# A mixture-of-experts block on one core: a waited-for clear after each scatter of GpSimd

## What is computed

```
x = x + attention(layernorm(x))      # linear attention, 16 heads of 8, RMS norms, rotary embedding
x = x + experts(layernorm(x))        # router: the best 2 of 8 experts of each token
x = x + mixing(layernorm(x))         # a recurrence over the 1024 tokens of each batch
x = x + experts(layernorm(x))
```

## Time and profile before

| | us |
|---|---|
| three runs, median | 1330.14 |
| lowest and highest | 1322.95, 1336.12 |
| profiled execution | 1346.64 |
| its span, first to last instruction | 1344.8 |
| busy: TensorE / VectorE / ScalarE / GpSimd | 855.2 / 918.4 / 659.9 / 623.3 |

### The profile page before, as it was taken

One profiled execution on the slowest core, in us unless ns is written; L12 is line 12 of the kernel. 1 busy time (PEld: TensorE's weight loads), 2 busy tenths in 40 slices (PEclk: granted clock), 3 DMA queues, 4 the chain that ended last, 5 costly groups with the idle time before them and its releaser, 6 DMA issues.

```text
span 1344.8 us, 21163 instructions
## 1 busy us (share of the span) xinstructions
PE 855.2 (64%) x5110; PEld 697.5 (52%) x5111; DVE 918.4 (68%) x2976; ACT 659.9 (49%) x1788; POOL 623.3 (46%) x597
## 2 busy tenths in 40 slices
PE   3777777742178887776457667657423777887850
PEld 1665566542177887765123333323223777876750
DVE  5688888645465655555299999999953565655657
ACT  3676666611154444444576766655322444444435
POOL 3024444433545554545215555675434555555440
PEclk9788877856599888899677787787655899889885
DMA  7022222212222222221311222211092222222239
GB/s 223 16 60 79 78 79 80 65 53 68 83 75 74 68 76 69 71 58 49 110 60 63 69 83 86 94 47 38 30 254 66 71 69 75 73 70 69 62 97 315
DMA packets 144880, 111.79 MB, mean 83 GB/s; under 512 B 15779, under 2 KB 135724, under 8 KB 144464
## 3 DMA queue, kind: packets, MB, share of 16 engines
q1 hardware_dynamic: 126928, 77.58, 20.6%
q0 software_dynamic: 17920, 33.88, 7.9%
HBM read 62.84 MB, written 50.64 MB: 84 GB/s over the span
## 4 chain that ended last, share of the span: by engine, by line
DVE 31%; PE 31%; issue 13%; ACT 7%; another core or an unknown queue 5%; POOL 5%; DMA 4%; DVEq 2%; ACTq 1%; SPq 0%; POOLq 0%
PE banks L965 8%; PE banks L946 5%; POOL queue_dram L508 4%; PE banks L948 4%; PE banks L947 4%; DVE rope_c L1414 3%; PE banks L828 2%; PE banks L854 2%; DVE stats L1095 2%; PE banks L955 2%; ACT gated L690 1%; DVE gated L1239 1%; DMA out<-xmid 1%; DVE tile_up L1253 1%
## 5 line engine op out<-in xcount | busy, mean ns | idle before, releaser
L519 POOL DMA_INDIRECT result_dram<-ytile,result_row x288 | 283.9, 986 | 274.3 <-DVE ytile L1259 191.8
L508 POOL DMA_INDIRECT queue_dram<-hffn,place_i x192 | 222.9, 1161 | 205.8 <-DVE place_i L1177 120.6
L946 PE MATMUL banks<-xt_parts,tile_up 128*128 128x256 f32 x584 | 185.8, 318 | 87.4 <-DVE tile_up L1253 81.6
L1239 DVE SCALAR_TENSOR_TENSOR gated<-banks,tile_bias,gated 128x256 f32<-128x256 f32 x292 | 127.8, 479 | 99.9 <-ACT gated L690 76.4
L965 PE MATMUL banks<-wdown_sb,gated 128*128 x1152 | 171.2, 297 | 20.6 <-DVE gated L1239 20.5
L947 PE MATMUL banks<-xt_parts,tile_up 128*128 128x256 f32 x584 | 172.9, 296 | 0.0
L948 PE MATMUL banks<-xt_parts,tile_up 128*128 128x256 f32 x584 | 172.7, 296 | 0.0
L946 PEld LDWEIGHTS banks<-xt_parts,tile_up 128*128 128x128 f32 x584 | 119.9, 205 | 100.7 <-DVE xt_parts L1248 61.9
L965 PEld LDWEIGHTS banks<-wdown_sb,gated 128*128 128x128 f32 x1152 | 157.8, 211 | 24.3 <-issue 24.2
L690 ACT ACTIVATE gated<-banks,tile_bias 128x256 f32<-128x256 f32 x292 | 121.9, 470 | 97.4 <-PE banks L948 70.2
L696 ACT ACTIVATE xt_parts<-banks 128x256 fp32r<-128x256 f32 x150 | 57.8, 386 | 215.2 <-PE banks L955 171.7
(11 more groups left out here) (210 smaller groups left out, 1986.8 us busy)
## 6 DMA issues: line engine op xcount, KB each, us to landing
xtiles<-queue_dram SPq DMA_DIRECT2D x160, 130.0 KB
qkv<-result_dram SPq DMA_DIRECT2D x24, 512.0 KB, 4.3
x_dram<-xres SPq DMA_DIRECT2D x32, 256.0 KB
result_dram<-ytile,result_row POOLq DMA_INDIRECT x288
xin<-x SPq DMA_DIRECT2D x16, 256.0 KB
xold<-x SPq DMA_DIRECT2D x16, 256.0 KB
expo<-w_up SPq DMA_DIRECT2D x2, 2048.0 KB, 9.3
xin<-x_dram SPq DMA_DIRECT2D x16, 256.0 KB
```

The source lines that it names most:

```text
L508: nc.gpsimd.indirect_dma_start(queue_dram, bass.IndirectOffsetOnAxis(ap=place_i[s][:, at:at + 1], axis=0), hffn[s][c][:, j, :], None).then ...
L519: nc.gpsimd.indirect_dma_start(result_dram, bass.IndirectOffsetOnAxis(ap=result_row[i][:, h:h + 1], axis=0), ytile[i][:, h, :], None, boun ...
L946: nc.tensor.matmul(ps_up[at][:, h, :], hi, xt_parts[at][:, 0, :], start=True, stop=False)
L1239: last = nc.vector.scalar_tensor_tensor(gated[at][:, h, :], ps_up[at][:, HCH + h, :], tile_bias[(i + 1) % STEP][:, HCH + h:HCH + h + 1], g ...
```

## The change

After each indirect DMA of GpSimd, in `scatter` and in `experts`, GpSimd sets a scratch tile of 16 columns to zero, waits until that is done and clears the semaphore. The seven waits of `pace` and the semaphore step that follows each are gone. The eight batches of the attention stage are one loop of four rounds.

```diff
+SPACER = 16
+        spacer = sb("spacer", [P, SPACER])
+        spaced = sem("spaced")
-            def pace(m, pair):
-                if pair == 1:
-                    pool.wait_ge(attn_turned[1], m + 1)
...
-                elif pair == 7:
-                    pool.wait_ge(h2_turned[0], m + 1)
-            def scatter(m, s, paced):
+            def space():
+                nc.gpsimd.memset(spacer[:], 0.0).then_inc(spaced, 1)
+                pool.wait_ge(spaced, 1)
+                pool.sem_clear(spaced)
+            def scatter(m, s):
...
                 for c in range(HALVES):
                     for j in range(TPC):
-                        if paced and c + j:
-                            pace(m, c * TPC + j)
-                            pool.sem_inc(place_taken, 1)
                         for k in range(TOPK):
...
                                 hffn[s][c][:, j, :], None).then_inc(queued[s][c], 16)
+                            space()
             def experts(f):
...
                                 ytile[i][:, h, :], None, bounds_check=NO_RESULT - 1, oob_is_err=False).then_inc(y_stored[i], 16)
+                            space()
...
-            with pool.Fori(0, 2) as n:
-                scatter(n * 2 + 1, 1, True)
-                scatter(n * 2 + 2, 0, True)
-            scatter(5, 1, True)
-            scatter(6, 0, False)
-            scatter(7, 1, False)
-            scatter(8, 0, False)
+            with pool.Fori(0, BATCH // 2) as n:
+                scatter(n * 2 + 1, 1)
+                scatter(n * 2 + 2, 0)
             experts(FIRST)
```

More of the change, by code:

```diff
@@ L568, in _ @@
                 next_sums(m - (BATCH - 1))
-                scatter(m, 0, False)
-            scatter(2 * BATCH - 1, 0, False)
-            scatter(2 * BATCH, 0, False)
+                scatter(m, 0)
+            scatter(2 * BATCH - 1, 0)
+            scatter(2 * BATCH, 0)
             experts(SECOND)
```

## The result

The kernel before took 1333.13 us (median of 4 runs, 1322.95 to 1338.26), the changed one 1500.97 us (4 runs, 1497.44 to 1502.11). The ratio is 1.127, 95% interval 1.119 to 1.134: slower, by more than the forecast's 1.105. The changed kernel's profiled execution took 1500.24 us (span 1498.4 us, granted clock 0.774), 153.6 us more than the 1346.64 us of the one before.

The account below looks back on a forecast made before the run. Experts were taken as bound by TensorE and VectorE passing tiles, mixing by VectorE, with attention's scatters mostly unwaited for. Terms summed to +141.3 us on 1346.64 us, ratio 1.105, forecasting 1470 us, range 1400 to 1530.

Parts of the forecast that it names:

- The cost of one clear: GpSimd's scatters: start to start 1.93 us in the queue (+0.67 us), 2.01 us for results (+0.73 us).
- Rival 1: GpSimd's sequencer runs ahead all the same, +0.28 us per scatter, experts stay hidden: 1357 us; chance 0.08.
- rival 3: The wait does not hold, clears finish beside the scatter's own work: 1334 us, no change; chance 0.05.
- Mixing stage: Sums queue behind the scatters: 9.0 us per batch, +45.0 us over five, +9.4 and +8.1 us for batches 15 and 16.
- Expert stages: GpSimd becomes the bound at 4.10 us per tile: +29.3 us in the first stage, +31.4 us in the second.
- rival 2: VectorE holds the clears up, in the experts its copy of weights: another 30 us, 1500 us; chance 0.10.
- Batch 8 to the first experts: Batch 8's last scatter starts 10.0 us later, less 1.9 us from a smaller hole and earlier start: +8.1 us.
- the hole after the first scatter: Batch 8's burst: the 1.98 us hole should shrink to a usual gap, as scatters 5 to 8 run in the loop.
- What bounded the experts before: Expert stages before the change: TensorE and VectorE pass tiles to each other, 3.70 us per tile.
- The dispatcher's price per instruction: GpSimd's software dispatcher: 0.04 us more per clear, some 17 us on the whole change; not used in the sum.
- Rival 4: Faster: spacing gives back ScalarE's 19.6 us of waits in attention batches 7 and 8: 1314 us; chance 0.04.
- The pair waits: Attention stage: five batches lose seven waits each, nothing there is waited for, so 0 us by itself.

Follow-up runs that it names:

- e1: The changed kernel without its clears in the experts, only those behind the queue's scatters kept: 1272.98 us, ratio 1.078 to a before of 1182.3 us.
- e2: The kernel before, pair waits kept, with waited-for clears behind the scatters of results alone: 1401.45 us, ratio 1.186 to a before of 1182.3 us.
- e4: The changed kernel with each clear waited for only ahead of the next one: 1183.08 us, ratio 1.001 to a before of 1182.3 us.
- e6: The changed kernel with each clear replaced by the sequencer's own semaphore count, wait and step kept: 1404.68 us, ratio 1.040 to a before of 1349.42 us.
- e7: The changed kernel with two waited clears after each scatter instead of one: 1626.69 us, ratio 1.205 to a before of 1349.42 us.
- e3: The changed kernel without any clears, so neither clears nor pair waits: 1181.85 us, ratio 1.001 to a before of 1182.3 us.
- e10: The kernel of e3 (neither clears nor pair waits) on another chip: 1401.18 us, ratio 1.041 to a before of 1347.21 us.
- e11: The kernel of e4 (clears waited for one later) on another chip: 1411.47 us, ratio 1.049 to a before of 1347.21 us.
- e5: The changed kernel as it is, run again in another set: 1501.90 us, ratio 1.112 to a before of 1349.42 us.
- e8: The changed kernel with a waited clear only after every second scatter: 1339.63 us, ratio 0.992 to a before of 1349.42 us.
- e9: The changed kernel with clears only after each second scatter of batches 1 to 7 and each fourth in the experts: 1289.82 us, ratio 0.959.

## Why the prediction held, and where its steps were off

The sum was 141.3 us and the profiled executions differ by 153.6. Up to the first result the forecast was 10.7 us too high, in the experts 23.8 us too low, and the rest is within 1.3 us. That two errors of opposite sign half cancel was luck; either alone would have left the total in the range. The ratio is also one for late chips, from whose trace it was worked out: for the other sort e1 and e2 add up to an estimate of some 1492 us, a ratio of 1.26, which no run tested.

**The cost of one clear: right.** I had 1.93 and 2.01 us from start to start; the rows above have 1.89 and 1.98. The mechanism, a stopped sequencer whose next issue lies in the open, is shown from three sides: the same clears without the stop cost nothing (e4), the same wait without an engine to wait for leaves the scatters where they were (e6), and a second clear costs 0.27 us, not another 0.7 (e7). Rival 1 and rival 3 fall with these.

**Mixing stage: right.** Place_i 9 to 15 grew by 53.7 us where 54.4 stood in the sum, 15 to 16 by 8.8 (8.1), the last burst by 8.8 (10.0). VectorE's wait for the sums (11.91 us ahead of 795.38) is the one forecast.

**Expert stages: the right bound, too small a size.** 293.1 us were forecast for the first stage, 305.9 measured. Over all 144 rows: 72 steps inside a tile have a median of 2.01 us, just the forecast's, but a mean of 2.10, with a single step of 4.43 us among them; 63 steps from tile to tile are 2.15 us instead of 2.09; and 8 steps at the end of a loop round are 2.49 us, for which the sum had nothing of its own. That is 6.1 + 3.5 + 3.2 = 12.8 us, of which 3.3 us are clears that VectorE held up (rival 2 below). The second stage is short by 11.0 us in the same way. These two terms are the whole miss upward, 23.8 us.

**Batch 8 to the first experts: wrong, and in the other direction.** I forecast +8.1 us; the first result came 2.6 us earlier. Two steps failed, and they nearly cancel. "Nothing there is waited for, so this gives 0 us by itself" missed that the spacing frees ScalarE and VectorE from late signals: place_i 8 comes 23.9 us earlier. And "it still fits, with 2 us to spare" was reckoned against batches 33.1 us apart; they now come 30.9 to 33.7 us apart, the last one 26.4 us. So GpSimd is full in attention: a batch's first scatter starts 4 us behind its place_i in batch 2 and 13.7 us in batch 8, which waits behind batch 7 (place_i 8 at 307.35, batch 7's last scatter at 318.75). GpSimd's rows, and VectorE's beside them:

```profile
318.75 0.97 POOL L497 DMA_INDIRECT queue_dram<-xtiles,place_i  x1 [1.02 <-issue]
319.07 4.42 DVE L1210 TENSOR_TENSOR up_lo<-expo,up_hi 128x4096 fp32r<-128x4096 f32 x1
...
321.03 3.30 POOL L497 DMA_INDIRECT queue_dram<-hffn,place_i  x1 [1.19 <-issue]
324.33 0.13 POOL L485 MEMSET spacer<- 128x16 f32 x1
327.72 0.97 POOL L497 DMA_INDIRECT queue_dram<-hffn,place_i  x1 [3.26 <-issue]
...
354.27 0.97 POOL L497 DMA_INDIRECT queue_dram<-hffn,place_i  x1 [0.80 <-POOL spacer L485]
370.89 1.00 POOL L509 DMA_INDIRECT result_dram<-ytile,result_row  x1 [15.53 <-DVE ytile L1246]
```

The burst starts 11.4 us earlier than in the earlier trace rows and is 33.24 us long instead of 24.90. These +8.3 us are what I had for the burst, but by another way. The first scatter lies beside a VectorE operation of 4.42 us and takes 3.30; in the kernel before a scatter of this burst met the same operation and took 5.19, so 1.9 us less are lost there now. And the hole after the first scatter, which I had expected to shrink from 1.98 us to a usual gap in the loop, grew to 3.26. The written-out code didn't make it: e3 has batch 8 in the loop and a hole of 1.99 us. Nor did VectorE's operation: in e7 the first scatter takes 0.97 us and the hole is 3.26 us again. What makes it is open.

**What bounded the experts before: wrong.** I read the 3.70 us of a tile as TensorE and VectorE passing tiles to each other. They can make one in 2.5 us, and GpSimd's two scatters allow 2.58 (e3: 191.4 us). The likely rest is late signals: without them the two stages are 142.6 us shorter (e3), and the view of waits over the whole run shows 81.8 us of this kind in them. That the other 61 us are waits that follow from these is argued, not shown. I had read this kind of wait in two attention batches only the earlier trace rows. It didn't spoil the sum, since the changed kernel's experts are bound by GpSimd alone and the forecast went from there; it did hide that with a smaller dose the change could have won.

**Rival 2** (VectorE holds the clears up) had a true mechanism at a fifth of its price. The mean of 0.152 us hides two kinds of clears. Of the 288 in the experts 40 lie beside VectorE's copy of weights (L1240), and 34 of these take 0.31 to 0.45 us; the 61 that lie beside L1226 alone take 0.14, like the others:

```profile
377.82 0.63 DVE L1240 CAST tile_up<-up_lo 128x512 fp32r x1
378.19 0.31 POOL L485 MEMSET spacer<- 128x16 f32 x1
```

Over both stages the 34 cost 6.3 us more than at 0.14 each, where the rival had 30. In the mixing stage six clears take 0.53 to 0.54 us, each beside L1365 or L1366. The page of the Trainium skill that speaks of a shared port lock (SBUF — State Buffer, section Who interferes with whom) has copies among the operations that can hold GpSimd up, and the 34 clears agree. It also lets a VectorE operation on two tiles in SBUF contend with GpSimd's reads; the scatter of 3.30 us beside VectorE's subtraction of 4.42 above agrees. The dispatcher's price per instruction, which I had set beside the sum as an estimate of 0.04 us more per clear (the Trainium skill, GPSIMD Engine Reference, section Instruction dispatch), doesn't show: the queue's steps came out at 1.89 or 1.90 us, under the sum's 1.93, not over it.

**Rival 4** had the mechanism and the wrong sign in total. Bursts do hold up signals to ScalarE and VectorE, spacing frees them, and in attention that is worth 24 us (19.6 forecast). My counter-argument, that these two batches run code for the first time, falls: e3 and e10 are one kernel and differ by 78 us at place_i 8 from chip to chip. At the dose of the change the experts and the mixing stage cost more than six times that gain.

**The pair waits** that I priced at 0 are worth 0 where signals are on time (e3) and most of 54 us in attention where they aren't (e10). The changed kernel has no late wait without them, so its clears seem to do their work, and the 0 came out right by another way than I gave; no run has clears and pair waits both in attention.

## What to carry to other kernels

A wait on one's own engine behind a DMA issue costs little for the instruction waited for and much for the next issue, which can't be prepared: 0.7 us per indirect DMA here. If a spacer or an ordering step is needed, wait for it one step later (e4: free; on a late chip e11 took 10 us more than e10). Look at the waits whose producer is done over the whole run, not in one window; where an engine issues DMAs back to back and such waits stand beside its bursts, a few stops, put where a queue has slack, can pay: clears after each second scatter in attention alone gave 1.7%, with every fourth scatter of the experts 4.1%. Time such a version on more than one chip: neither of these two was timed on one without late signals.

## What the runs showed of the hardware

- One kernel on several chips: 1182 us on one, 1333 to 1349 on the others, with each set's own runs within 1% or so. The slower sort has late signals in attention and in the experts; the four profiled versions of the faster set have none. Whether it is the chip, and why, is open.
- The late signals belong to runs of indirect DMAs 1.26 to 1.29 us apart: none with gaps of 0.80 us behind each scatter (changed, e5, e7) or behind each second one (e8), many with sixteen in a row (e10: up to 12.29 us, the longest until the burst ended), many again in the experts with four in a row (e9). An engine instruction between the scatters that leaves the spacing at 1.26 us doesn't help (e11). In the mixing stage bursts of sixteen had none, except in e11 (five waits of 3.5 to 4.9 us). Whether the length of the gap or the standing sequencer is what lets a signal through wasn't tried apart.
- VectorE can hold up a clear of 16 columns: 0.31 us or more beside its copy, 0.53 to 0.54 beside its operations on one tile and a number (L1365, L1366), 0.14 beside L1226. A scatter beside its subtraction of 4.42 us took 5.19 us in the kernel before and 3.30 in the changed one.
- The changed kernel took 1501.0 and 1501.9 us in two sets where the kernel before took 1333 and 1349. Both are of the slower sort; on the other it wasn't run.
